# Layer 2, last hidden tile: 64 gate and 64 up rows in one stationary, both experts' rows in one buffer

## What is computed

```
c     = sum over the token's 2 picks of where(pick == e, weight, 0)
h_e   = silu(x @ w_up.T + 2 * x @ up_A[e].T @ up_B[e].T) * (x @ w_gate.T + 2 * x @ gate_A[e].T @ gate_B[e].T)
ch    = c * h_e
out   = (sum_e ch) @ w_down.T + sum_e 2 * ch @ down_A[e].T @ down_B[e].T
```

## Time and profile before

| | |
|---|---|
| median of 3 runs | 519.8 us (518.56 to 524.3) |
| the profiled execution: device time | 519.72 us |
| its span, first to last instruction | 517.8 us |
| TensorE busy | 437.8 us, 85% of the span |
| VectorE busy | 377.9 us, 73% |
| GpSimd busy | 108.0 us, 21% |
| mean granted TensorE clock | 0.924 |

### The profile page before, as it was taken

How to read it: one execution, slowest core, us unless ns; L and a number is a source line. 1 busy time by engine, 2 the same in 40 slices (tenths; PEclk the granted TensorE clock), 3 DMA queues, 4 the chain that set the end, 5 groups by cost and what they waited for, 6 DMA issues and landing times.

```text
span 517.8 us, 5641 instructions
## 1 busy us (share of the span) xinstructions
PE 437.8 (85%) x2006; PEld 269.3 (52%) x2006; DVE 377.9 (73%) x663; ACT 195.2 (38%) x339; POOL 108.0 (21%) x65
## 2 busy tenths in 40 slices
PE   0796789987670899999999999999999999987572
PEld 0342444776470377899998997534434434322120
DVE  4999888797899798768666686375566773347975
ACT  4450155652221486321544824250010030146481
POOL 0000000000000297322000000047466654350000
PEclk9998788998965599999999999899999999999695
DMA  7910000710192127744754239020000000000001
GB/s 294 416 48 1 1 0 0 288 69 1 43 327 76 44 53 234 236 130 162 203 184 160 85 128 332 6 84 0 0 0 1 1 0 0 0 0 1 1 26 55
DMA packets 12093, 47.76 MB, mean 92 GB/s; under 512 B 2866, under 2 KB 5147, under 8 KB 9763
## 3 DMA queue, kind: packets, MB, share of 16 engines
q1 hardware_dynamic: 10914, 43.48, 24.0%
q0 software_dynamic: 1152, 3.93, 3.1%
HBM read 45.04 MB, written 2.37 MB: 92 GB/s over the span
## 4 chain that ended last, share of the span: by engine, by line
PE 69%; DVE 22%; issue 3%; ACT 3%; DMA 3%; SPq 0%; DVEq 0%
PE bank L1417 9%; PE bank L1391 8%; PE bank L1506 7%; PE bank L1515 7%; PE bank L1426 5%; PE bank L1543 3%; PE bank L1546 3%; PE bank L1279 3%; DMA const<-in_const 3%; PE bank L1321 2%; PE bank L1340 1%; PE bank L1311 1%; PE bank L1482 1%; DVE arena L903 1%; PE bank L1383 1%
## 5 line engine op out<-in xcount | busy, mean ns | idle before, releaser
L568 ACT ACTIVATE early<-bank 128x512 f32<-128x512 f32 (+1 forms) x24 | 14.3, 596 | 98.5 <-PE bank L1515 90.4
L1133 DVE TENSOR_TENSOR early<-early,bank 128x512 f32<-128x512 f32 (+1 forms) x24 | 16.4, 684 | 48.0 <-ACT early L568 47.6
L1391 PE MATMUL bank<-onehot,rows 128*128 128x512 f32 x192 | 51.4, 406 | 0.0
L341 POOL DMA_INDIRECT arena<-token_rows,arena x24 | 35.6, 1484 | 70.4 <-DVE arena L921 36.9
L1417 PEld LDWEIGHTS bank<-arena 128*96 128x96 f32 x512 | 44.2, 165 | 4.0 <-issue 3.9
L1506 PE MATMUL bank<-cT,arena 128*128 128x512 f32 (+1 forms) x96 | 46.2, 606 | 0.0
L1515 PE MATMUL bank<-arena 128*128 128x512 f32 (+1 forms) x96 | 45.8, 596 | 0.1
L1417 PE MATMUL bank<-arena 128*96 128x48 f32 x512 | 44.8, 248 | 0.3 <-issue 0.3
L1391 PEld LDWEIGHTS bank<-onehot,rows 128*128 128x128 f32 x192 | 33.9, 189 | 6.1 <-DVE onehot L952 0.3
L354 POOL TENSOR_TENSOR early<-early,arena 128x512 f32<-128x512 f32 (+1 forms) x12 | 28.0, 2333 | 41.8 <-DVE early L1133 41.8
L352 POOL TENSOR_TENSOR early<-early,arena 128x512 f32<-128x512 f32 (+1 forms) x12 | 15.1, 1262 | 103.0 <-DMA arena<-pair_weights 98.1
(11 more groups left out here) (315 smaller groups left out, 869.2 us busy)
## 6 DMA issues: line engine op xcount, KB each, us to landing
arena<-in_w_gate SPq DMA_DIRECT2D x8, 768.0 KB, 4.8
arena<-in_w_up SPq DMA_DIRECT2D x8, 768.0 KB, 7.8
arena<-in_w_down SPq DMA_DIRECT2D x8, 768.0 KB, 9.5
const<-in_const SPq DMA_DIRECT2D x1, 2122.5 KB, 13.1
arena<-in_wq SPq DMA_DIRECT2D x1, 2048.0 KB
arena<-in_wo SPq DMA_DIRECT2D x1, 2048.0 KB, 9.3
kT<-in_kT SPq DMA_DIRECT2D x2, 512.0 KB, 5.3
xT<-in_xT SPq DMA_DIRECT2D x1, 1024.0 KB, 8.5
```

The lines of the kernel that those rows point to most:

```text
L341: g.indirect_dma_start(xg[:, t % XRING, :], None, scratch[:, :], bass.IndirectOffsetOnAxis(ap=toki[:, t:t + 1].bitcast(U32), axis=0)).then ...
L1391: return mm(bank[2 * ct + ch][:], rows1[:, i % RRING, part, ct * P:(ct + 1) * P], onehot1[:, t, ch * CHUNK:(ch + 1) * CHUNK], start=False, ...
```

## The change

- Weights: up rows 0 to 639, gate rows 0 to 639, gate rows 640 to 703 and up rows 640 to 703 lie side by side in one tensor, `w_upgate2`, loaded by one DMA in place of two.
- Tiles 5 and 11: one stationary of 128 columns gives gate in partitions 0 to 63 and up in partitions 64 to 127 of one bank: two base matmuls instead of four. The LoRA matmuls keep 64 columns each and are written to their half of the bank.
- ScalarE and VectorE handle 64 partitions as before; for k = 0 the result goes to partitions 0 to 63, for k = 1 to 64 to 127 of the same `su`, `t` and `c` buffer. GpSimd makes no `mix` for these tiles. Its second product waits for `down2_done >= it` and counts two. VectorE's next tile waits for both products.
- `down2` of these tiles: the two down_A matmuls read rows 0 to 63 and rows 64 to 127; the two w_down matmuls read all 128 rows of `c1`, so that both experts are summed in the contraction. The last w_down and down_A rows are loaded twice, once for each half: two DMAs more.
- Semaphores: `wrb_in` becomes part of `const_in`, so that the waits for `const` are now for 32, both loads. `wd0_in` becomes part of `mlp0_in` (48), and `scores_done` and `vb_done` become `pick_done`.

```diff
-        wup2, wga2 = at(0, CT, H2), at(1408, CT, H2)
+        wug2 = at(0, CT, 2 * H2)
 ...
         def l2bufs(it):
+            if tail2(it):
+                return lbuf[0], lbuf[1], lbuf[3 + (it % 2)], lbuf[1], lbuf[3 + (it % 2)], None
             return lbuf[0], lbuf[1], lbuf[3 + (it % 2)], lbuf[2], lbuf[5 + (it % 2)], lbuf[7]
+        def tail2(it):
+            return it % H2T == H2T - 1
+        def rows2(it, k):
+            return slice(64 * k, 64 * k + 64) if tail2(it) else slice(0, P)
 ...
-            sp.dma_start(wrb[:], I["w_router"]...).then_inc(S("wrb_in"), 16)
+            sp.dma_start(wrb[:], I["w_router"]...).then_inc(S("const_in"), 16)
 ...
-            sp.dma_start(wd0, I["w_down0"]).then_inc(S("wd0_in"), 16)
+            sp.dma_start(wd0, I["w_down0"]).then_inc(S("mlp0_in"), 16)
 ...
+            sp.dma_start(wdn2[64:P, 5, :], I["w_down2b"]).then_inc(S("w2b_in"), 16)
+            sp.dma_start(adn[64:P, 5, :], I["down_Ab"]).then_inc(S("w2b_in"), 16)
 ...
                 pool.wait_ge(S("h2_ready"), 2 * it + 2)
-                g.tensor_tensor(c2[0:fw], t2[0:fw], c2b[0:fw, cc], ALU.mult).then_inc(S("ch_ready"), 1)
+                if tail2(it):
+                    pool.wait_ge(S("down2_done"), it)
+                    g.tensor_tensor(c2[r2], t2[r2], c2b[r2, cc], ALU.mult).then_inc(S("ch_ready"), 2)
+                    continue
+                g.tensor_tensor(c2[r2], t2[r2], c2b[r2, cc], ALU.mult).then_inc(S("ch_ready"), 1)
 ...
-                    s.activation(su[0:fw], bu[0:fw, :], ACT.Silu).then_inc(S("silu2"), 1)
+                    s.activation(su[rows2(it, k)], bu[64:P, :] if tail2(it) else bu[:], ACT.Silu).then_inc(S("silu2"), 1)
 ...
             def gate_product(it, k):
+                r = rows2(it, k)
+                up = bank[2 * (it % 2)][0:64, :] if tail2(it) else bank[2 * (it % 2) + 1][:]
                 dve.wait_ge(S("silu2"), 2 * it + k + 1)
                 if it >= 1:
-                    dve.wait_ge(S("ch_ready"), 3 * (it - 1) + k + 1)
-                v.tensor_tensor((t1, t2)[k][0:fw], su[0:fw], bank[2 * (it % 2) + 1][0:fw, :], ALU.mult).then_inc(S("h2_ready"), 1)
+                    dve.wait_ge(S("ch_ready"), 3 * (it - 1) + (2 if tail2(it - 1) else k + 1))
+                v.tensor_tensor((t1, t2)[k][r], su[r], up, ALU.mult).then_inc(S("h2_ready"), 1)
 ...
-            pe.wait_ge(S("const_in"), 16)
+            pe.wait_ge(S("const_in"), 32)
 ...
             def base2(it, z):
                 for ct in range(CT):
-                    mm(bank[2 * (it % 2) + z][0:fw, :], (wup2, wga2)[z][:, ct, f * P:f * P + fw], cT[...],
-                       start=(ct == 0), stop=False, skip_group_check=True)
+                    if not tail2(it):
+                        mm(bank[2 * (it % 2) + z][:], wug2[:, ct, z * 5 * P + f * P:z * 5 * P + (f + 1) * P], cT[...],
+                           start=(ct == 0), stop=False, skip_group_check=True)
+                    elif z == 0:
+                        mm(bank[2 * (it % 2)][:], wug2[:, ct, 10 * P:11 * P], cT[...],
+                           start=(ct == 0), stop=False, skip_group_check=True)
 ...
+                dst = bank[2 * (it % 2)][64 * (1 - z):64 * (2 - z), :] if tail2(it) else bank[2 * (it % 2) + z][:]
 ...
                 for k, cc_ in ((0, c1), (1, c2)):
-                    mm(bank[6 + k][:], adn[0:fw, f, :], cc_[0:fw], start=(f == 0), stop=(f == H2T - 1))
+                    mm(bank[6 + k][:], adn[rows2(it, k), f, :], cc_[rows2(it, k)], start=(f == 0), stop=(f == H2T - 1))
                 pe.wait_ge(S("ch_ready"), 3 * it + 3)
                 for ct in range(CT):
-                    last = mm(bank[4 + ct][:], wdn2[0:fw, f, ct * P:(ct + 1) * P], mix[0:fw], start=(f == 0), stop=False)
+                    last = mm(bank[4 + ct][:], wdn2[:, f, ct * P:(ct + 1) * P], c1 if tail2(it) else mix, start=(f == 0), stop=False)
```

More of the change, by code:

```diff
@@ L253, in _ @@
             sp.dma_start(const[:], I["const"]).then_inc(S("const_in"), 16)
-            sp.dma_start(wrb[:], I["w_router"].rearrange("(o c) -> o c", o=1).to_broadcast([P, C])).then_inc(S("wrb_in"), 16)
+            sp.dma_start(wrb[:], I["w_router"].rearrange("(o c) -> o c", o=1).to_broadcast([P, C])).then_inc(S("const_in"), 16)
             sp.dma_start(bias8, I["qkv_b"]).then_inc(S("qkvw_in"), 16)
@@ L294, in _ @@
             sp.wait_ge(S("ffn1_done"), NG - 1)
-            for dst, name in ((gw2, "gate_w2"), (wup2, "w_up2"), (wga2, "w_gate2"), (aup, "up_A"), (aga, "gate_A"), (bup, "up_B"), (bga, "gate_B")):
+            for dst, name in ((gw2, "gate_w2"), (wug2, "w_upgate2"), (aup, "up_A"), (aga, "gate_A"), (bup, "up_B"), (bga, "gate_B")):
                 sp.dma_start(dst, I[name]).then_inc(S("w2a_in"), 16)
@@ L347, in _ @@
                 ch, f = divmod(it, H2T)
-                fw = H2W[f]
                 su, t1, c1, t2, c2, mix = l2bufs(it)
                 cc = slice(ch * CHUNK, (ch + 1) * CHUNK)
+                r1, r2 = rows2(it, 0), rows2(it, 1)
                 pool.wait_ge(S("h2_ready"), 2 * it + 1)
-                g.tensor_tensor(c1[0:fw], t1[0:fw], c1b[0:fw, cc], ALU.mult).then_inc(S("ch_ready"), 1)
+                g.tensor_tensor(c1[r1], t1[r1], c1b[r1, cc], ALU.mult).then_inc(S("ch_ready"), 1)
                 pool.wait_ge(S("h2_ready"), 2 * it + 2)
-                g.tensor_tensor(c2[0:fw], t2[0:fw], c2b[0:fw, cc], ALU.mult).then_inc(S("ch_ready"), 1)
+                if tail2(it):
[3 more added lines that the diff above has]
+                g.tensor_tensor(c2[r2], t2[r2], c2b[r2, cc], ALU.mult).then_inc(S("ch_ready"), 1)
                 pool.wait_ge(S("ch_ready"), 3 * it + 2)
@@ L357, in _ @@
                     pool.wait_ge(S("down2_done"), it)
-                g.tensor_tensor(mix[0:fw], c1[0:fw], c2[0:fw], ALU.add).then_inc(S("ch_ready"), 1)
+                g.tensor_tensor(mix[r1], c1[r1], c2[r1], ALU.add).then_inc(S("ch_ready"), 1)
         @block.scalar
@@ L560, in _ @@
             for it in range(NCH * H2T):
-                fw = H2W[it % H2T]
                 su, t1, c1, t2, c2, mix = l2bufs(it)
@@ L727, in _ @@
                 den_scans(1, 0, b)
-            dve.wait_ge(S("scores_done"), 1)
+            dve.wait_ge(S("pick_done"), 1)
             step(v.tensor_copy(scr, bank[0][0:B, 0:T]))
@@ L732, in _ @@
                 step(v.match_replace(scr, m8a, scr, PICKED))
-            dve.wait_ge(S("const_in"), 16)
+            dve.wait_ge(S("const_in"), 32)
             v.tensor_copy(spread4.rearrange("p (b j) -> p b j", b=B), ident[0:B, 0:B].unsqueeze(2).to_broadcast([B, B, TOP]))
@@ L738, in _ @@
             v.tensor_tensor(rank4, scr, picked, ALU.mult).then_inc(S("rank_ready"), 1)
-            dve.wait_ge(S("vb_done"), 1)
+            dve.wait_ge(S("pick_done"), 2)
             for b in range(B):
@@ L760, in _ @@
             sumsq(xs, 1)
-            dve.wait_ge(S("wrb_in"), 16)
             step(v.tensor_tensor(dl, xs, wrb[:], ALU.mult))
@@ L1235, in _ @@
                               start=(b == 0 and ct == 0), stop=(b == B - 1 and ct == CT - 1))
-            last.then_inc(S("scores_done"), 1)
+            last.then_inc(S("pick_done"), 1)
             tokens_to_rows([1, 2, 3, 4], 0)
@@ L1246, in _ @@
             pe.wait_ge(S("rank_ready"), 1)
-            mm(bank[5][:, 0:T], spread4, rank4, start=True, stop=True).then_inc(S("vb_done"), 1)
+            mm(bank[5][:, 0:T], spread4, rank4, start=True, stop=True).then_inc(S("pick_done"), 1)
             for i in range(NT):
@@ L1314, in _ @@
             pe.wait_ge(S("hT0_ready"), 4)
-            pe.wait_ge(S("mlp0_in"), 32)
+            pe.wait_ge(S("mlp0_in"), 48)
             for j in range(2):
@@ L1323, in _ @@
                     last.then_inc(S(name), 1)
-            pe.wait_ge(S("wd0_in"), 16)
             for f in range(F0T):
@@ L1503, in base2 @@
                 ch, f = divmod(it, H2T)
-                fw = H2W[f]
                 for ct in range(CT):
-                    mm(bank[2 * (it % 2) + z][0:fw, :], (wup2, wga2)[z][:, ct, f * P:f * P + fw], cT[:, ct, ch * CHUNK:(ch + 1) * CHUNK],
-                       start=(ct == 0), stop=False, skip_group_check=True)
+                    if not tail2(it):
+                        mm(bank[2 * (it % 2) + z][:], wug2[:, ct, z * 5 * P + f * P:z * 5 * P + (f + 1) * P], cT[:, ct, ch * CHUNK:(ch + 1) * CHUNK],
+                           start=(ct == 0), stop=False, skip_group_check=True)
+                    elif z == 0:
+                        mm(bank[2 * (it % 2)][:], wug2[:, ct, 10 * P:11 * P], cT[:, ct, ch * CHUNK:(ch + 1) * CHUNK],
+                           start=(ct == 0), stop=False, skip_group_check=True)
             def lora2(it, k, z):
@@ L1514, in lora2 @@
                     pe.wait_ge(S("zm_ready"), 4 * ch + (2 * k + z + 1 if ch == 0 else 2 * k + 2))
-                last = mm(bank[2 * (it % 2) + z][0:fw, :], (bup, bga)[z][:, f * P:f * P + fw],
```

(14 more changed lines are left out.)

1 line of the change is left out of this document (removed).

## The result

The changed kernel takes 518.2 us in the median of 20 runs (513.15 to 525.0), the kernel before 519.92 (518.11 to 524.3, 20 runs). With the runs left out in which TensorE's clock was low more often, the ratio is 0.9905, 95% interval 0.9876 to 0.9934: 4.9 us faster, 3.4 to 6.4. The forecast was 2.0 us faster. Most of the rest of this document is about the missing 2.9 us. The profiled execution of the changed kernel (521.87 us, span 519.9) is longer than that of the kernel before although the changed layer is shorter in it, because TensorE's clock was low for longer. So the two spans can't be compared, and the reading goes by stretches.

The account below looks back on a forecast made before the run. The prediction took layer 2 to be bound by TensorE's number of passes. Its terms, -1.1 - 1.72 + 0.85 = -1.97, took 519.72 to 517.75, forecast as 517.8 us (0.4% faster), range 515.9 to 520.6.

Parts of the forecast that it names:

- array shape: Narrow matmuls in columns or rows 64 to 127: no row shows their cost; taken as 0, at most 0.6 us lost.
- The first rival: Narrow LoRA matmuls overlap in different columns, three slots of 0.43 instead of four: 1.3 us more gain, 516.5 us; chance 0.28.
- tile 5, base matmuls: Four passes fewer in tile 5: 1.1 us gained, not 1.72, as TensorE then waits for VectorE's gate product of tile 4.
- tile 11, base matmuls: Four passes fewer in tile 11: the whole 1.72 us gained, as the needed gate product ends almost 4 us earlier.
- LoRA pairs side by side: Three narrow LoRA pairs on the chain in tiles 5 and 11: no overlap counted in the forecast, 0.
- later start: TensorE's first matmul also waits for `wrb`: 0.85 us later, all carried to the end; lower bound 0.43.
- the number of passes at 0.43: Layer 2: each tile takes TensorE 10.30 us, 24 passes at 0.43 us, nothing but matmuls.
- this gain moves through VectorE's chain: From tile 6's second gate product to `bias_down2(0)`: TensorE starts this chain through ScalarE, so tile 5's 1.1 us lives on.
- `cond3` moves with it: Before `gu3(0)`: `cond3`'s last part follows tile 10's gate product, so it moves too; TensorE's idle stays near 2.2 us.
- GpSimd's later product: Tiles 5 and 11: GpSimd's second product waits for `down2` and takes the sum's place; costs nothing.
- the cover of `masked_down(1)`: After tile 11: `down2(11)` ends near 469.0, `masked_down(1)` starts at 469.91, so 0.9 us of cover.
- The absorbed rival: VectorE holds the chain at both places, so only the start's loss is left: 520.6 us; chance 0.12.

Follow-up runs that it names:

- e1: The changed kernel with both LoRA matmuls of tiles 5 and 11 written to the upper half of the bank; ratio 0.9980 to the kernel before.
- e5: The kernel before with gate's 64 rows in partitions 64 to 127 of its own bank and base calls alternating between up and gate; ratio 0.9873.
- e6: The changed kernel with both down_A matmuls of tiles 5 and 11 reading rows 0 to 63; ratio 0.9907 to the kernel before.
- e7: The changed kernel with VectorE's next products (after tiles 3 and 6) between the two long steps of `round_weights`; ratio 0.9837 to the kernel before.
- e4: The changed kernel with four 64-column base calls in tiles 5 and 11, gate's two then up's two; 73.1 us from second LoRA pair to `bias_down2(0)`, as unsplit.
- e11: The kernel before with only gate's 64 rows moved to partitions 64 to 127, old order; 38.95 us from `bias_down2(0)` to `gu3(0)`, against 40.6.
- e10: The kernel before with e5's gate placement and alternating calls plus e7's VectorE order; 70.59 us from second LoRA pair to `bias_down2(0)`, 0.85 above e7.

## Why the prediction was wrong

**The step that failed: array shape.** The prediction said that what no row shows is a narrow matmul in columns or rows 64 to 127, and took 0. e1 shows that it is the term that was missing: 0.86 us for each pair of narrow LoRA matmuls in different columns. Three pairs are on the chain: the second of tile 5 (S1), the first of tile 11 (S2), the second of tile 11 (S3). That is 2.6 us, nearly as large as the base matmuls' gain. The first rival, at 0.28, had the mechanism and its places right, and half the size: it took one slot of four off each pair, 0.43, where two go, 0.86, since all four passes overlap in twos (1.0 us for the four, 0.86 and a change of shape). The Trainium skill had it: "TensorE: Matmul & The Clock Gate", Part 3, gives concurrent matmuls in distinct column groups, and the runs agree with it, 0.86 off a pair of 1.72. The prediction said that by that page the sum would be this rival's, 516.5; matmuls that are concurrent as a whole would have given 515.2. I had weighed it, and kept the forecast on rows that could not show it: all narrow passes of the kernel before stand in the same columns.

With it the sum comes near the measured time:

```
term                              forecast   measured, where
tile 5, base matmuls                -1.1     -1.05   (S1 -1.91 less the pair's 0.86)
tile 11, base matmuls               -1.72    -1.70   (S2 + S3 -3.42 at high clock (e5), less two pairs)
LoRA pairs side by side              0       -2.58   (three times 0.86; 2.56 by e1's stretches)
later start                         +0.85    +0.70   (14 profiles, about 0.25 either way)
sum                                 -1.97    -4.6    measured by time -4.9 (-6.4 to -3.4)
```

That it comes as near as 0.3 is in part luck, for the clock is not in it. From `gu3(0)` to the end of the span, the kernel before took 60.5 us. The profiled execution of the changed kernel took 61.5, and e6, which differs from it only off the chain and had a higher clock, 58.6. The sum has 1.1 of gain there, and the clock alone moved it between 1.9 of gain and 1.0 of loss.

**Right:** that the number of passes at 0.43 bounds the layer; that tile 5's base matmuls give 1.1 and not 1.72, since VectorE's product behind `round_weights` is next (387.58 and 388.32 in the chain, a wait of 1.4 us, longer than the 0.6 forecast, as the 0.86 of tile 5's first side-by-side pair fell into it too); that this gain moves through VectorE's chain to `bias_down2(0)`; that tile 11 gives the whole; that `cond3` moves with it (TensorE's idle before `gu3(0)` 2.44, before 2.23); that GpSimd's later product costs nothing, in both tiles. It was quicker than forecast, 1.26 us and not 2.0 in tile 5, and the cover of `masked_down(1)` 1.6 us and not 0.9, the rest from down_A side by side.

**The start** was sized well, for a reason that holds only on average. In the one profile of the changed kernel it seemed to cost 0.06.

**The absorbed rival** fell: both places moved. But its observation, that VectorE holds tile 4, was the pointer to e7, which took 3.3 us more out of S1.

**The range** (515.9 to 520.6) holds the median of all 20 runs, 518.2; by the ratio, the changed kernel stands at 515.0, below it. The chances were for a change under 1%, and it is 0.95%.

## What to carry to other kernels

When a matmul has 64 columns or 64 rows, ask where its neighbours stand before anything else: putting one of two into the other half of the array took 0.86 us off each fp32 pair in columns (0.85 in rows), for the change of a start partition. A trace in which all narrow matmuls stand at 0 says nothing about that price; there a bound from its rows must include the overlap of everything that could overlap. And after TensorE's share has become shorter, look again at who releases it: reordering VectorE gave 1.0 us of S1 before and 3.3 after.

## What the runs showed of the hardware

- The two halves of the array's columns run as two streams, not only neighbour beside neighbour: a pass in the free half started beside the one four places ahead of it, in both cases seen (e4, e11). Program order of gate, gate, up, up cost nothing (S2 38.04); up, up, LoRA, gate, gate, LoRA cost 0.9 (38.95).
- Narrow fp32 passes side by side each take as long as alone (0.43 apart), in columns (the changed kernel, 1.87 us for six passes, against e1, 2.72) as in rows (1.06 against 1.91 us for the down_A pair, e7 and e10).
- TensorE's granted clock fell to 0.50 for 6.8 us in layer 1 in one execution and not in another of the same work, at 3.7 us of cost (the changed kernel's TensorE is 0.2 ahead of the kernel before at 185 and 3.5 behind at 209). The changed kernel's 20 runs go with the mean granted clock: 0.919 to 0.926 in the eight under 515.2 us, 0.901 to 0.904 in the four above 524, though two at 518 had 0.921 and 0.923. What sets it was not settled.
